# The last tile's GELU layer in halves on two engines and two banks, two tiles' reads of integers on VectorE, and the instruction orders set anew

## What is computed

```python
def _L0_cond_ref(x, h0, Wx, Wh, b):
    xW = jnp.einsum('ntd,dh->nth', x, Wx) + b
    def step(prev_h, xw_t):
        next_h = jnp.tanh(prev_h @ Wh + xw_t)
        return (next_h, next_h)
...
for e in range(E):                       # 16 experts, 4 of 16 weighted, the others by zero
    we = jnp.sum(weights * (indices == e), axis=-1)
    h = jax.nn.silu(x2 @ W1[e].T + b1[e]) * (x2 @ W3[e].T + b3[e])
    y = y + (h @ W2[e].T + b2[e]) * we[:, None]
...
def bitlinear(x, W, b):
    w_scale = jnp.clip(jnp.mean(jnp.abs(W)), EPS, None)
    Wq = _ste(W, jnp.clip(jnp.round(W / w_scale), -1.0, 1.0) * w_scale)
    x_scale = jnp.clip(jnp.max(jnp.abs(x), axis=-1, keepdims=True), EPS, None)
    xq = _ste(x, jnp.clip(jnp.round(x * (QB / x_scale)), -QB - 1.0, QB) * (x_scale / QB))
    return jnp.einsum('bnd,hd->bnh', xq, Wq) + b
h = bitlinear(x, W1, b1)                 # 128 -> 512
h = jax.nn.gelu(h, approximate=False)
return bitlinear(h, W2, b2)              # 512 -> 128
...
x = x + _L0_ffn_ref(_L0_cond_ref(x, cond_1024, ...), ...)
x = x + _L1_ffn_ref(_L1_cond_ref(x, cond_1024, L1_cond_weight), ...)
```

## Time and profile before

| | us |
|---|---|
| median of 3 runs | 147.68 |
| lowest and highest of them | 146.3, 149.26 |
| the profiled execution | 145.98 |
| its span, first to last instruction | 144.2 |
| TensorE matmuls busy in it | 139.8 |
| VectorE busy | 104.0 |
| ScalarE busy | 82.9 |
| GpSimd busy | 33.7 |
| granted TensorE clock, mean | 0.999 of full speed |

### The profile page before, as it was taken

How to read it: one execution, slowest core, us unless ns; L and a number is a source line. 1 busy time by engine, 2 the same in 40 slices (tenths; PEclk the granted TensorE clock), 3 DMA queues, 4 the chain that set the end, 5 groups by cost and what they waited for, 6 DMA issues and landing times.

```text
span 144.2 us, 3607 instructions
## 1 busy us (share of the span) xinstructions
PE 139.8 (97%) x1149; PEld 131.8 (91%) x1149; DVE 104.0 (72%) x399; ACT 82.9 (58%) x277; POOL 33.7 (23%) x86
## 2 busy tenths in 40 slices
PE   6999999999999999999999999999999999999993
PEld 2598899999999999999999999999999987999992
DVE  4300298989987688529999537999785999799741
ACT  3022366577874355545565554489858614869871
POOL 3000047299905460000151000006110002301100
PEclk9999999999999999999999999999999999999999
DMA  4999200270035000088000059200006910000111
GB/s 78 374 379 380 98 0 0 55 241 6 0 113 182 6 2 5 5 259 324 6 0 0 2 123 368 100 0 0 5 5 149 402 40 0 18 0 7 39 52 36
DMA packets 6693, 13.90 MB, mean 96 GB/s; under 512 B 1586, under 2 KB 3219, under 8 KB 6291
## 3 DMA queue, kind: packets, MB, share of 16 engines
q1 hardware_dynamic: 6384, 13.61, 28.5%
q10 hardware_dynamic: 290, 0.07, 0.2%
HBM read 13.08 MB, written 0.59 MB: 95 GB/s over the span
## 4 chain that ended last, share of the span: by engine, by line
PE 84%; DVE 7%; issue 3%; DMA 3%; ACTq 1%; DVEq 0%; ACT 0%
PE a L1048 19%; PE b L1048 17%; PE y_ps L1157 13%; PE rnn L1089 9%; PE y_ps L1060 8%; DVE hid L978 3%; DMA h_sb<-h0T 3%; PE b L1157 2%; DVE hid L969 2%; PE m_ps L1089 2%; PE a L1184 2%; PE y_ps L1152 1%; PE rnn L1163 1%; PE rnn L1036 1%; PE m_ps L1107 1%
## 5 line engine op out<-in xcount | busy, mean ns | idle before, releaser
L969 DVE SCALAR_TENSOR_TENSOR hid<-b,b_sb,gate_u 128x256 f32<-128x256 f32 (+1 forms) x80 | 33.7, 424 | 11.5 <-PE b L1048 5.8
L741 ACT ACTIVATE hs<-rnn 128x8 f32<-128x8 f32 x112 | 19.8, 177 | 33.0 <-PE rnn L1089 30.6
L1089 PEld LDWEIGHTS rnn<-hs,wh_sb 128*128 128x128 f32 x224 | 34.8, 191 | 0.8
L765 ACT ACTIVATE gate_u<-a,b_sb 128x256 f32<-128x256 f32 (+1 forms) x80 | 33.5, 427 | 3.1 <-DVE hid L969 1.9
L1157 PE MATMUL y_ps<-hid,w_sb 128*128 128x128 f32 (+1 forms) x160 | 32.6, 321 | 0.0
L1089 PE MATMUL rnn<-hs,wh_sb 128*128 128x8 f32 x224 | 32.6, 218 | 0.0
L978 DVE TENSOR_TENSOR hid<-hid,we_bc 128x128 f32<-128x128 f32 (+1 forms) x80 | 24.7, 349 | 0.7 <-DMA we_bc<-we_dram 0.7
L1157 PEld LDWEIGHTS y_ps<-hid,w_sb 128*128 128x128 f32 x160 | 24.2, 191 | 1.0
L1060 PE MATMUL y_ps<-warm_sb 128*128 128x256 bf16 x108 | 16.8, 271 | 0.0
L1048 PE MATMUL a<-hs_hi,w_lo 128*128 128x256 f32 x48 | 16.4, 341 | 0.0
L1048 PE MATMUL a<-hs_hi,w_hi 128*128 128x256 f32 x48 | 15.2, 316 | 0.0
(11 more groups left out here) (152 smaller groups left out, 269.4 us busy)
## 6 DMA issues: line engine op xcount, KB each, us to landing
we_bc<-we_dram SPq DMA_DIRECT2D x12, 512.0 KB, 5.8
we_bc<-we_dram SPq DMA_DIRECT2D x8, 256.0 KB, 4.5
w_sb<-W1T SPq DMA_DIRECT2D x1, 1024.0 KB, 6.1
w_sb<-W3T SPq DMA_DIRECT2D x1, 1024.0 KB, 8.4
w_sb<-W2T SPq DMA_DIRECT2D x1, 1024.0 KB, 7.7
out<-out_sb SPq DMA_DIRECT2D x8, 64.0 KB, 1.5
xT_sb<-xT SPq DMA_DIRECT2D x1, 448.0 KB, 4.0
f_sb<-F1T SPq DMA_DIRECT2D x1, 256.0 KB, 6.1
```

The lines of the kernel that those rows point to most:

```text
L741: act.activation(hs[:, cols], rnn_bank(n * BATCH, BATCH), ACT.Tanh).then_inc(h_ready, 1)
L765: act.activation(gate_u[:, n % U_RING, 0:w], a_ps[n % 2][:, 0:w], ACT.Silu, bias=b1_sb[:, e:e + 1]).then_inc(silu_ready, 1)
L969: dve.scalar_tensor_tensor(out=hid[:, n % H_RING, 0:w], in0=b_ps[n % 2][:, 0:w], scalar=b3_sb[:, e:e + 1], in1=gate_u[:, n % U_RING, 0:w], ...
L1089: pe.matmul(rnn_bank(n * BATCH, BATCH), wh_sb[:], prev, start=False, stop=True, skip_group_check=True).then_inc(z_ready, 1)
```

## The change

- **Tile 7 in halves** of 256 columns. HP_READ becomes HP_FIRST and HP_READ (both VectorE, one bank), GELU becomes GELU_FIRST and GELU (both ScalarE), AMAX2 becomes AMAX2_FIRST, which puts the first half's maximum in an added 513th column, and AMAX2 over the second half and that column. Rounding goes on both engines at once: ROUND2 on ScalarE for the first half, ROUND2_B on VectorE for the second. T2 transposes two blocks into R1 and T2_B two into m_ps; T2_READ (ScalarE) and T2_READ_B (VectorE) read them; OUT waits for the second read only in front of its third matmul.
- **T2_READ of tiles 0 and 2** moves from ScalarE to VectorE.
- **The start**: the bias matmul into a_ps goes into the planned order, behind recurrence step 2, and the SEED copies follow it.
- **Orders**: all of `LIFT` and the slips and margins are new, the recurrence is assumed to start at 5.6 instead of 5.0, and SILU 21 must stand behind TANH 40. `WARM_STEPS` is 0, so the WARM operations that the diff also adds aren't issued.
- `weighted_on_dve` is written otherwise and gives the same split.

```diff
+READ2_ON_DVE = (0, 2,)
+POOL_SUMS = (0, 1)
+LAST = TILES - 1
 GELU_BATCHES = [(0, 1), (2, 3), (4,), (5,), (6,), (7,)]
 PASSES = {1: 1, 2: 3}
 MAX_PASSES = 3
 START_KEEPS = 6
+WARM_STEPS = 0
...
-    if kind in ("SCORES", "WT", "XT", "Q"):
+    if kind in ("SCORES", "WT", "XT", "Q", "T2_B"):
...
+def read2_on_dve(i):
+
+    return i in READ2_ON_DVE
+
+
 def weighted_on_dve(u):
 
-    return SUMS[u // EXPERTS][1] > 1 or u // EXPERTS >= LAST_CHUNK or u % 2 == 0
+    return u // EXPERTS not in POOL_SUMS or u % 2 == 0
...
-RNN_START = 5.0
-PE_SLIP, ACT_SLIP, KEEP_SLIP, MARGIN = 0.27, 0, 0.09, 0.13
+RNN_START = 5.6
+PE_SLIP, ACT_SLIP, KEEP_SLIP, MARGIN = 0.1, 0.03, 0.08, 0.05
 
 LIFT = {
-    "HIDDEN": 133, "W": -57, "Y": -49, "FIN": 71, "FIN_READ": -48, "XF": -86, "XT": -16, "XB": 31,
-    "GATE": 90, "SCORES": 198, "SCORES_READ": 51, "TANH_S": 126, "EXP": 127, "SIG1": 170, "SIG2":
-    286, "WT": 258, "WT_READ": 143, "OUT_READ": -113, "ROUND1": 27, "SILU": 63, "T2": -86, "SPLIT":
-    117, "OUT": -7, "Z": 128, "RECIP1": -82, "AMAX2": -83, "HP": -14, "HP_READ": 55, "SCALE1": 132,
-    "XO": 305, "X": 99, "AMAX1": 76, "Q": 129, "Q_READ": 206, "B": 86, "DEQ2": -19, "GELU": 52,
-    "SCALE2": -27, "RECIP2": -27, "ROUND2": 66, "T2_READ": -34, "SETUP": 36, "TERNARY": 71, "A":
-    102, "DEQ1": 116}
-
+    "HIDDEN": 343, "W": -273, "Y": -117, "FIN": -119, "FIN_READ": -148, "XF": -45, "XT": -60, "XB":
+    24, "GATE": 118, "SCORES": 207, "SCORES_READ": -105, "TANH_S": 165, "EXP": 236, "SIG1": 120,
+    "SIG2": 268, "WT": 215, "WT_READ": 92, "OUT_READ": -159, "ROUND1": 54, "SILU": 94, "T2": -185,
+    "SPLIT": 166, "OUT": -81, "Z": 185, "RECIP1": 57, "AMAX2": -47, "HP": 52, "HP_READ": 44,
+    "SCALE1": 181, "XO": 444, "X": 232, "AMAX1": 122, "Q": 180, "Q_READ": 139, "B": 51, "DEQ2": -79,
+    "GELU": -119, "SCALE2": -68, "RECIP2": -68, "ROUND2": 56, "T2_READ": -60, "SETUP": 71,
+    "TERNARY": -20, "A": 130, "DEQ1": 99, "GELU_FIRST": -4, "AMAX2_FIRST": -88, "ROUND2_B": -77,
+    "T2_B": 66, "T2_READ_B": -35, "HP_FIRST": -64}
+
+
+
+TURNS = [(("SILU", 21), ("TANH", 40))]
...
+    put("PE", "BIAS", 0, [(0.14, 0.007), (0.12, 0.007)], RESULT, [], [("RNN", 2)])
...
+        if i == LAST:
+            put("DVE", "HP_FIRST", i, 0.36, 0.50, [("HP", i), ("DEQ1", i)])
+            put("DVE", "HP_READ", i, 0.36, 0.50, [("HP", i), ("DEQ1", i)], same("HP_READ", i) + [("HP_FIRST", i)])
+        else:
+            put("DVE", "HP_READ", i, 0.66, 0.80, [("HP", i), ("DEQ1", i)], same("HP_READ", i))
         batch = next(b for b in GELU_BATCHES if i in b)
-        put("ACT", "GELU", i, 0.54, 0.69, [("HP_READ", k) for k in batch] + [("TANH", STEPS - 1)], same("GELU", i), "gelu")
-        put("DVE", "AMAX2", i, 0.60, 0.74, [("GELU", i)], same("AMAX2", i))
+        ready = [("HP_READ", k) for k in batch] + [("TANH", STEPS - 1)]
+        if i == LAST:
+            put("ACT", "GELU_FIRST", i, 0.33, 0.48, [("HP_FIRST", i)], same("GELU", i), "gelu")
+            put("ACT", "GELU", i, 0.33, 0.48, ready, [("GELU_FIRST", i)], "gelu")
+            put("DVE", "AMAX2_FIRST", i, 0.33, 0.47, [("GELU_FIRST", i)], same("AMAX2", i))
+            put("DVE", "AMAX2", i, 0.33, 0.47, [("GELU", i), ("AMAX2_FIRST", i)])
+        else:
+            put("ACT", "GELU", i, 0.54, 0.69, ready, same("GELU", i), "gelu")
+            put("DVE", "AMAX2", i, 0.60, 0.74, [("GELU", i)], same("AMAX2", i))
         put("DVE", "SCALE2", i, 0.065, 0.20, [("AMAX2", i)], same("SCALE2", i))
         put("DVE", "RECIP2", i, 0.07, 0.21, [("SCALE2", i)], same("RECIP2", i))
         put("POOL", "DEQ2", i, 0.25, 0.35, [("SCALE2", i)], same("DEQ2", i))
-        put("ACT", "ROUND2", i, 0.71, 0.86, [("RECIP2", i)], same("ROUND2", i))
-        put("PE", "T2", i, [(LOAD, 0.107)] * 4, RESULT + 0.05, [("ROUND2", i)] + late("T2"), same("T2", i) + two_ago("OUT"))
-        put("ACT", "T2_READ", i, 0.58, 0.75, [("T2", i)], same("T2_READ", i))
-        put("PE", "OUT", i, [(0.06, 0.06)] * 4, RESULT + 0.05, [("T2_READ", i), ("XB", i)], same("OUT", i))
+        half = i == LAST
+        put("ACT", "ROUND2", i, 0.40 if half else 0.71, 0.56 if half else 0.86, [("RECIP2", i)], same("ROUND2", i))
+        put("PE", "T2", i, [(LOAD, 0.107)] * (2 if half else 4), RESULT + 0.05, [("ROUND2", i)] + late("T2"),
+            same("T2", i) + two_ago("OUT"))
+        behind = same("T2_READ", i) if i and read2_on_dve(i) == read2_on_dve(i - 1) else []
+        if read2_on_dve(i):
+            put("DVE", "T2_READ", i, 0.60, 0.74, [("T2", i)], behind)
+        else:
+            put("ACT", "T2_READ", i, 0.33 if half else 0.58, 0.50 if half else 0.75, [("T2", i)], behind)
+        if half:
+            put("DVE", "ROUND2_B", i, 0.30, 0.44, [("RECIP2", i)])
+            put("PE", "T2_B", i, [(LOAD, 0.107)] * 2, RESULT + 0.05, [("ROUND2_B", i)], [("T2", i)])
+            put("DVE", "T2_READ_B", i, 0.30, 0.44, [("T2_B", i)])
...
                     b = bank_of("T2", n)
                     wait_filled(act, "T2", n)
-                    act.activation(q2T[:, n % 2, :], banks[b][:], ACT.Identity, bias=minus_magic[:]).then_inc(freed[b], 1)
+                    cols = first_half(n)
+                    act.activation(q2T[:, n % 2, cols], banks[b][:, cols], ACT.Identity, bias=minus_magic[:]).then_inc(freed[b], 1)
                 if kind == "ROUND2":
 
                     act.wait_ge(inv2_ready, n + 1)
-                    act.activation(hp[:, n, :], hp[:, n, :], ACT.Identity, bias=magic[:],
+                    cols = first_half(n)
+                    act.activation(hp[:, n, cols], hp[:, n, cols], ACT.Identity, bias=magic[:],
                                    scale=inv_step[:, 2 * n + 1:2 * n + 2]).then_inc(rounded2, 1)
+                if kind == "GELU_FIRST":
+                    act.wait_ge(hp_first, 1)
+                    act.activation(hp[:, n, FIRST], hp[:, n, FIRST], ACT.Gelu).then_inc(gelu_first, 1)
                 if kind == "GELU":
                     wait_read(act, "HP", n)
-                    act.activation(hp[:, n, :], hp[:, n, :], ACT.Gelu).then_inc(gelu_ready, 1)
+                    cols = second_half(n)
+                    act.activation(hp[:, n, cols], hp[:, n, cols], ACT.Gelu).then_inc(gelu_ready, 1)
...
+                    cols = slice(0, HIDDEN)
+                    if n == LAST:
+                        after(("AMAX2_FIRST", n))
+                        cols = slice(HIDDEN // 2, HIDDEN + 1)
+                    mark(dve.tensor_reduce(amax[:, one], hp[:, n, cols], AX_X, ALU.max, apply_absolute_value=True), (kind, n))
+                if kind == "AMAX2_FIRST":
+                    dve.wait_ge(gelu_first, 1)
+                    mark(dve.tensor_reduce(hp[:, n, MAXIMUM], hp[:, n, FIRST], AX_X, ALU.max, apply_absolute_value=True), (kind, n))
+                if kind == "ROUND2_B":
+                    dve.wait_ge(inv2_ready, n + 1)
+                    dve.tensor_scalar(hp[:, n, SECOND], hp[:, n, SECOND], inv_step[:, 2 * n + 1:2 * n + 2], MAGIC,
+                                      ALU.mult, ALU.add).then_inc(rounded2_b, 1)
+                if kind == "T2_READ":
+                    b = bank_of(kind[:2], n)
+                    wait_filled(dve, "T2", n)
+                    dve.tensor_scalar(q2T[:, n % 2, :], banks[b][:], MAGIC, None, ALU.subtract).then_inc(freed[b], 1)
+                if kind == "T2_READ_B":
+                    wait_filled(dve, "T2_B", n)
+                    dve.tensor_scalar(q2T[:, n % 2, SECOND], m_ps[:, FIRST], MAGIC, None, ALU.subtract).then_inc(freed[M], 1)
...
+                    cols = second_half(n)
+                    dve.scalar_tensor_tensor(out=hp[:, n, cols], in0=banks[b][:, cols], scalar=deq[:, 2 * n:2 * n + 1],
+                                             in1=fb1_bc[:, cols], op0=ALU.mult, op1=ALU.add).then_inc(freed[b], 1)
+                if kind == "HP_FIRST":
+                    wait_filled(dve, "HP", n)
+                    dve.wait_ge(deq_ready[0], n + 1)
+                    dve.scalar_tensor_tensor(out=hp[:, n, FIRST], in0=banks[bank_of("HP", n)][:, FIRST], scalar=deq[:, 2 * n:2 * n + 1],
+                                             in1=fb1_bc[:, FIRST], op0=ALU.mult, op1=ALU.add).then_inc(hp_first, 1)
...
-            pe.matmul(a_ps[0][:, 0:1], bh_row[:], ones_row[:, 0:1], start=True, stop=True, skip_group_check=True).then_inc(marked, 1)
...
+                if kind == "BIAS":
+                    pe.matmul(a_ps[0][:, 0:1], bh_row[:], ones_row[:, 0:1], start=True, stop=True, skip_group_check=True).then_inc(marked, 1)
...
-                    for k in range(HB):
+                    for k in range(HB // 2 if n == LAST else HB):
                         last = pe.transpose(banks[b][:, k * P:(k + 1) * P], hp[:, n, k * P:(k + 1) * P], ident[:])
                     last.then_inc(filled[b], 1)
+                if kind == "T2_B":
+                    pe.wait_ge(rounded2_b, 1)
+                    wait_free(pe, kind, n)
+                    for k in range(HB // 2):
```

(5 more changed lines are left out.)

32 lines of the change are left out of this document (21 added, 11 removed).

## The result

The changed kernel takes 154.14 us (median of 4 runs, 153.11 to 154.84) against 146.99 (4 runs, 145.57 to 149.26) for the kernel before: a ratio of 1.053, 95% interval 1.046 to 1.060. It is slower by 7 us, where I forecast 1.7 us less. The profiled execution took 154.34 us with a span of 152.6; that of before took 145.98 with 144.2.

The account below looks back on a forecast made before the run. TensorE's work was taken to bound the kernel up to 131 us, then tile 7's hand-over chain. -0.4 - 0.6 - 0.1 - 0.15 + 0 - 0.4 = -1.65 us, from 147.68 to 146.0 us; forecast's own range 145.2 to 146.9, overall 144.0 to 148.6.

Parts of the forecast that it names:

- Start, 0: Ahead of the input products: moved bias matmul and seed copies stay hidden, since step 0 waits for h0; 0, at most +0.1 us.
- Orders set anew, -0.4: Up to 131 us: new orders win only fillers and idle time, TensorE's work staying the same; -0.4 us, bounds -1.4 and +1.4.
- More fillers than 10: Sign of a wrong forecast: many more TensorE fillers than 10 between 17 and 131 us.
- Reads of tiles 0 and 2, -0.15: Integer reads moved to VectorE: tile 0's 0, tile 2's frees tile 7's rounding; -0.15 us, bounds -0.42 and +0.2.
- L1021 to the maximum, -0.4: Tile 7's bias and scale to its maximum's end: halves overlap across engines; -0.4 us of 2.42, at best -0.65.
- Behind the second reciprocal, -0.6: Tile 7's last rounding to output: shorter rounding and read, two final products not waiting; -0.6 us, bounds -0.25 and -0.65.
- Output ahead of the step, -0.1: Tail: tile 4's output no longer goes ahead of tile 7's step, as outputs' priority falls; -0.1 of 0.14 us.
- The weighed rule: Tile 7's half maxima: fixed instruction costs favour 512 elements or more; would lose 0.16 us where the sum gains 0.27.
- SILU 21 behind TANH 40, 0: A turn on ScalarE inside the recurrence: 0, at most one tanh's 0.18 us.
- third rival: GELU of tiles 0 and 1 lands among the SILUs, stopping TensorE; 149.0 us at full price, chance 0.13.
- first rival: Queues in the tail eat the halves' gain: -0.2 us, 147.5 us in all, chance 0.2.
- What would show it: Signs of being right: tile 7's residual sum near 131.07, tail 9.9 us, last GELU's end to last output's end 3.6.

Follow-up runs that it names:

- the third kernel of the experiments: The changed kernel with nine instead of six wide fillers ahead of the recurrence; 148.14 us, ratio to before 1.005.
- the first 5.6: The changed kernel with the one-column bias matmul back ahead of the recurrence; 147.62, 152.06, 153.97 and 154.39 us, the profiled one being the 147.62.

## Why the prediction was wrong

- **Start, 0 (bounds 0 and +0.1): the step that failed.** I asked when VectorE's seeds come free and whether h0 gates step 0, and costed the moved matmul and the seed copies as hidden work. The two fillers fewer in step 2 and the input products that come earlier, which the planned order brings, had no term, and TensorE's own rate I left at "full granted clock", from a column that doesn't show it. Measured: +6.38 us in the changed kernel's profile, 0.97 of it up to step 0 and 5.41 in the 16 steps behind it, most of which ran at the lower rate; and 2 of 4 runs at +6 us or more when only this start is put into the kernel before. The rows that could have warned me stood in the trace of before: its wide fillers get shorter at about 4.0 us, just ahead of step 0, and its own runs lie 3 us apart. I took that spread as noise of the measurement; the profiles of the kernels above put the rise at 4 to 20 us, and that gives it a likely cause.
- **Orders set anew, -0.4 (bounds -1.4 and +1.4).** Sign wrong. With the start undisturbed they cost -0.03 + 1.64 = +1.61 us, just outside the bounds. In the five other profiles with these orders and these reads the stretch behind the recurrence is 1.36 to 1.58 us over before's in four and 2.29 in one (the bias matmul back at the start), so the size isn't sharp, but the sign is. I wrote that TensorE's work stays the same up to 131 us, so only fillers and idle time could move. But that border is tile 7's residual sum, and work can cross it: nine down-projections out of the recurrence to behind it, seven transposes or products out of the tail to ahead of it. "More fillers than 10" was no test for that: 13 within the recurrence and none behind it were found, against 12 and 2 in the kernel before by the same count.
- **Reads of tiles 0 and 2, -0.15 (bounds -0.42 and +0.2).** The price of one was right (0.68 us on VectorE, 0.67 to 0.69 on ScalarE). Their worth has no single value: +1.07 by hand in before's orders, +3.2 in the tail when planned anew with before's priorities, -0.6 (-0.74 in the tail, +0.13 ahead) in the changed orders. No read stands between the first reciprocal and the first rounding any more, as foreseen; a copy (L837, 143.16) now does, for 0.12 us. But tile 2's read on VectorE (140.78) and an output (142.23) now stand ahead of tile 7's first maximum: the reciprocal ends 2.91 us behind the residual sum instead of 2.42, the rounding starts 3.07 behind instead of 2.88. That +0.19 is what the bound of +0.2 described, not the -0.15 that I took.
- **L1021 to the maximum, -0.4.** Measured 2.04 against 2.42: -0.38. One read does stand ahead of both halves, and two outputs of VectorE between the pieces, so the best case of -0.65 wasn't reached.
- **Behind the second reciprocal, -0.6.** Measured 2.78 against 3.28: -0.50. **Output ahead of the step, -0.1:** from the maximum's end to the rounding's start 0.49 against 0.55, -0.06. From tile 7's residual sum to bias and scale it is 5.04 against 4.88, +0.16. The tail's four figures give -0.78 where the sum had -1.1 without the reads.
- **The weighed rule.** By the Trainium skill's page VectorE: DVE Perf Modes (The TRN2 errata) two half maxima cost more than one whole. The trace agrees on that (0.41 + 0.41 against 0.69) and the step gained all the same, since the first is covered.
- **SILU 21 behind TANH 40, 0**, and the **third rival** (GELU among the SILUs): the table loads start at 102.75 and 105.33, the first directly behind the last tanh at 102.55. It didn't happen. Nor did the first rival; the tail gained.
- **What would show it.** Tile 7's residual sum within 1 us of 131.07: it came at 140.24. The tail 9.9: 10.35. From the last GELU's end 3.6: 150.59 - 146.60 = 3.99. The first of these was the right alarm, but I had no case behind it: the chance of 0.05 for over 3 us named an order, not the rate.

The change as a whole would have cost 1.1 to 1.4 us with an undisturbed start (the span above, and the medians with nine fillers in both). It adds 5 to 6 us by making common an execution that none of before's 76 runs had. Which of the start's instructions delay the rise, and how, stays open. The halves alone take 0.6 us off the tail, in all four profiles that have them with before's orders and reads (10.51 or 10.52 against 11.13). That is too little for runs that lie at levels 2 us apart to prove: 0.988 (0.979 to 0.997) of before in 4 runs, 0.999 (0.992 to 1.006) in 6 with nine fillers, and 0.993 (0.986 to 1.000) in 12 with the input products spread, where the highest run is 148.51 instead of 149.76 beside it.

## What to carry to other kernels

Before costing a move among the first instructions of a kernel, look at what one and the same matmul takes there and later: if its durations change, TensorE's rate is part of the sum, and a few matmuls fewer or moved can cost more than they take. When runs of one kernel lie at levels and not around a mean, find the cause of the levels first; a change can move the kernel to another level. And where an engine is full up to a border, count what a new order carries across the border in both directions, since work that is the same in total isn't the same on each side.

## What the runs showed of the hardware

- TensorE's rate rose at 4.0 to 19.5 us after the start, in kernels whose first 4 us are the same instructions: before 4.0, the third kernel of the experiments 5.3, the first 5.6, halves alone 9.7, changed with the old start 12.7, before with the bias matmul late 13.6, changed 19.5. Until it rises matmuls of 256 bf16 columns start 0.21 us apart (1.2 GHz), then 0.11 (2.4 GHz). In the changed kernel no two matmuls start more than 0.35 us apart from 6.64 to 19.5 us, so it was not an idle TensorE that stayed at the lower level. The Trainium skill's page TensorE: Matmul & The Clock Gate (Part 1) says that the chip's monitor runs free of the kernel's start, so that the moment of the rise varies, by half a microsecond. The traces agree that it varies, but by up to 15.5 us here (19.5 - 4.0), between kernels whose orders differ behind the first 4 us.
- Where the rise before step 0 was missed, it came latest (19.5 us) in the start whose steps 4 to 6 hold two fp32 input products each and whose step 2 has two fillers fewer, and sooner with the products spread among fillers (9.5 and 12.5 us in two profiles; no run of 12 above 148.51 us). Which property of these matmuls does it wasn't tested.
- A clock column of 1.00 can stand over a stretch at half rate, where the trace's clock records begin only later (19.53 us in the changed kernel).
- VectorE's wait for the transfer of the gates (we_bc) differs between profiles: 0.7 us in all in that of before and none to 1.2 in others with before's orders, 2.8 in that of the changed kernel and 0.6 to 2.3 in six others with its orders. Within a kernel it wasn't measured twice, so how much of it is chance is open.
